# Rows turned into columns by VectorE in blocks of 32, in place of TensorE transposes, in a metaformer layer with routed experts

## The reference, cut to what matters

```python
x = x + conv_attention(layer_norm_over_channels(x))        # 8 images, 64 channels, 256 pixels
t = to_tokens(x)                                           # 2048 tokens of 64 channels
n = layer_norm(t)
probs = softmax(n @ router_w.T)                            # 8 experts
top, idx = top_k(probs, 2); top = top / (top.sum(-1) + 1e-9)
h = silu(n @ w1[e].T) * (n @ w3[e].T)                      # hidden width 682
t = t + sum over the two chosen e of  top * (h @ w2[e].T)
x = from_tokens(t)
```

## Time and profile before

| | us |
|---|---|
| median of 3 runs (lowest, highest) | 174.03 (172.21, 176.63) |
| the profiled execution | 174.15 |
| its span, first to last instruction | 172.4 |
| busy in the span: PE, DVE, ACT, POOL | 146.7, 97.1, 71.4, 86.2 |
| mean granted clock of TensorE, share of full speed | 0.959 |

### The profile page before, as it was taken

One profiled execution on the slowest core, in us unless ns is written; L12 is line 12 of the kernel. 1 busy time (PEld: TensorE's weight loads), 2 busy tenths in 40 slices (PEclk: granted clock), 3 DMA queues, 4 the chain that ended last, 5 costly groups with the idle time before them and its releaser, 6 DMA issues.

```text
span 172.4 us, 4966 instructions
## 1 busy us (share of the span) xinstructions
PE 146.7 (85%) x1725; PEld 119.7 (69%) x1725; DVE 97.1 (56%) x364; ACT 71.4 (41%) x141; POOL 86.2 (50%) x114
## 2 busy tenths in 40 slices
PE   1589889886979899919999999999999999984772
PEld 1356757344446688818898999999999999874262
DVE  1636695884765799828363656455554645433050
ACT  2347666123144352502363636363645454542011
POOL 2695227887777722777262625344443526356000
PEclk9999999998799999985899999999999999999789
DMA  4999200108815955945969795969688930000435
GB/s 135 335 297 302 69 0 19 31 15 268 327 38 99 322 220 201 345 110 162 389 181 378 222 391 148 399 177 364 224 268 319 296 145 30 11 25 19 116 135 122
DMA packets 19894, 33.00 MB, mean 191 GB/s; under 512 B 7692, under 2 KB 13101, under 8 KB 19869
## 3 DMA queue, kind: packets, MB, share of 16 engines
q1 hardware_dynamic: 16732, 29.55, 52.2%
q0 software_dynamic: 2272, 2.35, 4.1%
q10 hardware_dynamic: 864, 0.79, 1.4%
HBM read 25.55 MB, written 7.13 MB: 190 GB/s over the span
## 4 chain that ended last, share of the span: by engine, by line
POOL 35%; issue 32%; PE 11%; DVE 11%; DMA 5%; ACT 3%; POOLq 1%; SPq 0%; DVEq 0%; ACTq 0%
POOL ys L375 21%; POOL xs L366 13%; DMA y_in<-ys 2%; PE psum L1129 2%; DVE hid L833 2%; ACT xn L431 2%; PE psum L934 2%; DVE xrows L638 1%; DMA ys<-y_out,y_row 1%; PE psum L945 1%; PE psum L905 1%; DMA proj<-projections 1%; POOL rstd_t L356 1%; DVE rows L600 1%; PE psum L900 1%
## 5 line engine op out<-in xcount | busy, mean ns | idle before, releaser
L375 POOL DMA_INDIRECT ys<-y_out,y_row x39 | 37.3, 957 | 44.3 <-DVE y_out L845 35.2
L833 DVE TENSOR_TENSOR hid<-psum,act_sb 128x512 f32<-128x512 f32 (+1 forms) x50 | 33.9, 677 | 33.0 <-ACT act_sb L509 32.6
L1056 PE MATMUL psum<-x_cols,weights 64*128 64x128 f32 x390 | 49.6, 279 | 0.4 <-DVE hid L833 0.4
L1058 PE MATMUL psum<-x_cols,weights 64*128 64x128 f32 x390 | 49.7, 279 | 0.0
L1056 PEld LDWEIGHTS psum<-x_cols,weights 64*128 64x128 f32 x390 | 45.5, 187 | 3.9 <-issue 2.6
L1058 PEld LDWEIGHTS psum<-x_cols,weights 64*128 64x128 f32 x390 | 45.6, 187 | 0.0
L366 POOL DMA_INDIRECT xs<-xrows,pos x32 | 32.1, 1003 | 17.5 <-issue 8.7
L509 ACT ACTIVATE act_sb<-psum 128x512 f32<-128x512 f32 (+1 forms) x50 | 29.3, 587 | 25.3 <-PE psum L1056 24.9
L1084 PE MATMUL psum<-hid,weights 128*64 128x128 f32 x468 | 30.6, 287 | 0.0
L1084 PEld LDWEIGHTS psum<-hid,weights 128*64 128x64 f32 x468 | 27.8, 144 | 1.9 <-issue 0.3
L978 PE MATMUL psum<-ones,before 128*128 128x512 bf16 x67 | 18.8, 418 | 3.5 <-issue 3.5
(11 more groups left out here) (147 smaller groups left out, 173.1 us busy)
## 6 DMA issues: line engine op xcount, KB each, us to landing
weights<-experts SPq DMA_DIRECT2D x39, 565.0 KB, 5.5
xs<-zeros SPq DMA_DIRECT2D x4, 1040.0 KB, 11.6
x_in<-xs SPq DMA_DIRECT2D x39, 32.5 KB
ys<-y_out,y_row POOLq DMA_INDIRECT x39
xs<-xrows,pos POOLq DMA_INDIRECT x32, 4.0
y_in<-ys ACTq DMA_DIRECT2D x2, 256.0 KB, 4.6
y_in<-ys SPq DMA_DIRECT2D x2, 256.0 KB, 4.3
x_sb<-x_tok SPq DMA_DIRECT2D x1, 384.0 KB, 3.6
```

The lines of the kernel that those rows point to most:

```text
L375: nc.gpsimd.indirect_dma_start(ys, bass.IndirectOffsetOnAxis(ap=y_row[:, j:j + 1], axis=0), y_out[:, i % RING, h, :], None).then_inc(y_sca ...
L833: nc.vector.tensor_tensor(live(i, hid[:, i % 2, s, :]), live(i, H3_BANK[g % 3]), live(i, act_sb[:, g % 3, :]), ALU.mult).then_inc(hid_done, 1)
L1056: first_ = nc.tensor.matmul(H1_BANK[g % 2][:, src], weights[0:C, slot, P * s:P * (s + 1)], x_cols[0:C, i % 2, src], start=True, stop=True)
L1058: second_ = nc.tensor.matmul(H3_BANK[g % 3][:, src], weights[C:P, slot, P * s:P * (s + 1)], x_cols[C:P, i % 2, src], start=True, stop=True)
```

## The change

Rows are no longer spread over 128 partitions, one row each, but over 32 partitions, four rows each: partition p of a subtile holds rows 4p to 4p + 3, which lie one behind the other in DRAM. `turn_x` is now DVE's: four transposes in 32x32 blocks write the four parts of `x_cols` (two halves of the channels, each twice) straight from `x_in`, and four small copies bring the row numbers of each part to their partitions; in the last phase a predicated copy follows. PE's transposes, ACT's copy, `x_pairs` and `X_BANK` are gone, and with them two filler matmuls. A column of a subtile now stands for another row than before (column 32r + p for row 4p + r), and `occupancy` compares accordingly in four parts.

SP reads four entries of a table with one load, and the order of its DMAs is the same from quad 2 on: table, rows, weights. The turn of quad 2 moves from behind the third product of quad 1 to behind the fifth.

The diff (one line that only drops a bank's name is left out):

```diff
--- before.py
+++ after.py
@@ -54,7 +54,7 @@
 YROWS = PARK + NS * SUB
 WQUADS = 3
 WSLOTS = WQUADS * QUAD
-TURNED_AT = {0: 1, 1: 4}
+FOLD = SUB // 32
 XRING = 4
 RING = 4
 ZW = E * CAP * RW // (QUARTERS * P * 8)
@@ -144,11 +144,11 @@
         jump = sb("jump", [P, E - 1])
         row_at = sb("row_at", [P, NS])
         limit = sb("limit", [P, NS])
-        table = sb("table", [P, 2, NS], I32)
+        table = sb("table", [P, 2, NQ * QUAD], I32)
         keep = sb("keep", [P, NS], I32)
 
-        x_in = sb("x_in", [P, XRING, QUAD, RW])
-        x_pairs = sb("x_pairs", [P, 2, QUAD, 2, C])
+        x_in = sb("x_in", [32, XRING, QUAD, FOLD, RW])
+        ids = sb("ids", [P, NS], I32)
         x_cols = sb("x_cols", [P, 2, QUAD * SUB])
         act_sb = sb("act_sb", [P, 3, BLK])
         hid = sb("hid", [P, 2, STEPS, BLK])
@@ -193,8 +193,8 @@
 
         w_loaded = [sem(f"w_loaded{i}") for i in range(WSLOTS)]
         x_in_loaded = [sem(f"x_in_loaded{i}") for i in range(XRING)]
-        x_paired, y_row_ready, hid_cleared = sem("x_paired"), sem("y_row_ready"), sem("hid_cleared")
-        x_turned, x_cols_ready = sem("x_turned"), sem("x_cols_ready")
+        y_row_ready, hid_cleared = sem("y_row_ready"), sem("hid_cleared")
+        x_cols_ready = sem("x_cols_ready")
         h1_done, h3_done = sem("h1_done"), sem("h3_done")
         silu_done, hid_done, hid_used = sem("silu_done"), sem("hid_done"), sem("hid_used")
         y_copied, y_turned, y_out_ready = sem("y_copied"), sem("y_turned"), sem("y_out_ready")
@@ -278,28 +278,28 @@
                     sp.dma_start(weights[:, slot, :], experts[bass.ds(owners[h], 1)].rearrange("o p c -> p (o c)")
                                  ).then_inc(w_loaded[slot], 16)
 
+            def entries(i, kind, most):
+                quad = table[0:1, kind, QUAD * i:QUAD * i + len(members(i))]
+                return nc.values_load_multi_w_load_instructions(quad, engines=(mybir.EngineType.SP,), min_val=0, max_val=most)[1]
+
             def owners_of(i):
-                return [sp.value_load(table[0:1, 0, QUAD * i + h:QUAD * i + h + 1], min_val=0, max_val=E - 1)
-                        for h in members(i)]
+                return entries(i, 0, E - 1)
 
             def rows_of(i):
-                return [sp.value_load(table[0:1, 1, QUAD * i + h:QUAD * i + h + 1], min_val=0, max_val=E * CAP - SUB)
-                        for h in members(i)]
+                return entries(i, 1, E * CAP - SUB)
 
             def load_rows(i, at):
                 if i >= XRING:
                     sp.wait_ge(y_row_ready, i - XRING + 1)
-                    sp.wait_ge(x_paired, i - XRING + 1)
                 for h in members(i):
-                    sp.dma_start(x_in[:, i % XRING, h, :], xs[bass.ds(at[h], SUB), :]).then_inc(x_in_loaded[i % XRING], 16)
+                    sp.dma_start(x_in[:, i % XRING, h, :, :],
+                                 xs[bass.ds(at[h], SUB), :].rearrange("(p r) c -> p r c", r=FOLD)).then_inc(x_in_loaded[i % XRING], 16)
 
             def landed(p):
                 sp.wait_ge(dispatched[p], 16 * TPP * K_TOP * (KNOWN[p] - (KNOWN[p - 1] if p else 0)))
 
             sp.wait_ge(owners_ready, 1)
-            for h in members(0):
-                owner = sp.value_load(table[0:1, 0, h:h + 1], min_val=0, max_val=E - 1)
-                sp.dma_start(weights[:, h, :], experts[bass.ds(owner, 1)].rearrange("o p c -> p (o c)")).then_inc(w_loaded[h], 16)
+            load_weights(0, owners_of(0))
             sp.wait_ge(table_ready, 1)
             early_rows, second_owners = [rows_of(0), rows_of(1)], owners_of(1)
             landed(0)
@@ -307,18 +307,13 @@
             load_rows(1, early_rows[1])
             load_weights(1, second_owners)
             for p in range(1, PHASES):
-                sp.wait_ge(owners_ready, p + 1)
-                opening = quads_of(p)[0]
-                if opening < WQUADS:
-                    load_weights(opening, owners_of(opening))
                 sp.wait_ge(table_ready, p + 1)
                 for i in quads_of(p):
-                    at = rows_of(i)
-                    if i == opening:
+                    at, owners = rows_of(i), owners_of(i)
+                    if i == quads_of(p)[0]:
                         landed(p)
                     load_rows(i, at)
-                    if i >= WQUADS:
-                        load_weights(i, owners_of(i))
+                    load_weights(i, owners)
 
             all_scattered(sp)
             for q in range(0, QUARTERS, 2):
@@ -399,7 +394,7 @@
             count_up(steps_sub[:], [[SUB, MOST]], SUB, 0)
             for p in range(PHASES):
                 count_up(slot_at[:, OPENED[p]:OPENED[p + 1]], [[SUB, OPENED[p + 1] - OPENED[p]]], 0, 0)
-            count_up(slot_no[:], [[1, 1]], 0, 1)
+            count_up(slot_no[:], [[1, 1]], 0, FOLD)
             count_up(y_row[:], [[SUB, NS]], PARK, 1)
             nc.gpsimd.affine_select(out=upto[:], in_=upto[:], compare_op=ALU.is_ge, fill=0.0, base=0,
                                     pattern=[[1, E], [-1, E]], channel_multiplier=0).then_inc(tables_made, 1)
@@ -494,12 +489,6 @@
                     kq_copy(p + 2)
             nc.scalar.preload_act_table(ACT.Silu)
 
-            def columns(i):
-                act.wait_ge(x_turned, i + 1)
-                if i >= 2:
-                    act.wait_ge(h3_done, STEPS * (i - 1))
-                nc.scalar.copy(live(i, x_cols[:, i % 2, :]), live(i, X_BANK)).then_inc(x_cols_ready, 1)
-
             def silu(g):
                 i, s = divmod(g, STEPS)
                 act.wait_ge(h1_done, g + 1)
@@ -524,14 +513,11 @@
                     ins = nc.scalar.copy(y_cols[0:odd, i % 2, whole:whole + P], Y_BANK[0:odd, whole:whole + P])
                 ins.then_inc(y_copied, 1)
 
-            columns(0)
             for i in range(NQ):
                 if i >= 1:
                     y_copy(i - 1)
                 for s in range(STEPS):
                     silu(STEPS * i + s)
-                    if s == TURNED_AT.get(i, 0) and i + 1 < NQ:
-                        columns(i + 1)
             y_copy(NQ - 1)
             nc.scalar.preload_act_table(ACT.Exp)
             act.wait_ge(shifted, 1)
@@ -727,8 +713,11 @@
                 chain(nc.vector.tensor_reduce(limit[:, own], starts[:, own, :], AX.X, ALU.add))
                 chain(nc.vector.scalar_tensor_tensor(out=limit[:, own], in0=limit[:, own], scalar=left[:, 0:1],
                                                      in1=row_at[:, own], op0=ALU.add, op1=ALU.subtract))
-                nc.vector.tensor_tensor(keep[:, own], limit[:, own], slot_no[:].to_broadcast([P, n]), ALU.is_gt
-                                        ).then_inc(keep_ready, 1)
+                for r in range(FOLD):
+                    part = slice(32 * r, 32 * (r + 1))
+                    nc.vector.scalar_tensor_tensor(out=keep[part, own], in0=limit[part, own], scalar=float(r * (SUB - 1)),
+                                                   in1=slot_no[part, :].to_broadcast([32, n]), op0=ALU.add, op1=ALU.is_gt
+                                                   ).then_inc(keep_ready, 1)
 
             def gate_shifts():
                 dims = [P, TILES, E]
@@ -779,20 +768,26 @@
             x_logits(0)
             scales(3)
 
-            def pair_up(i):
+            def turn_x(i):
                 slot, n = i % XRING, len(members(i))
+                own = slice(QUAD * i, QUAD * i + n)
                 dve.wait_ge(x_in_loaded[slot], landed_in(i))
                 if i >= 2:
-                    dve.wait_ge(x_turned, i - 1)
-                nc.vector.tensor_copy(x_pairs[:, i % 2, 0:n, :, :], x_in[:, slot, 0:n, 0:C].unsqueeze(2)
-                                      .to_broadcast([P, n, 2, C])).then_inc(x_paired, 1)
-                own = slice(QUAD * i, QUAD * i + n)
-                ids = x_in[:, slot, 0:n, ID].bitcast(I32)
-                if own.stop <= OPENED[PHASES - 1]:
-                    nc.vector.tensor_copy(y_row[:, own], ids).then_inc(y_row_ready, 1)
-                else:
-                    dve.wait_ge(keep_ready, 1)
-                    nc.vector.copy_predicated(y_row[:, own], keep[:, own], ids).then_inc(y_row_ready, 1)
+                    dve.wait_ge(h3_done, STEPS * (i - 1))
+                for part in range(4):
+                    c = 32 * (part % 2)
+                    ins = nc.vector.transpose(live(i, x_cols[32 * part:32 * (part + 1), i % 2, :]
+                                                   ).rearrange("p (h r t) -> p h r t", r=FOLD, t=32),
+                                              x_in[:, slot, 0:n, :, c:c + 32])
+                ins.then_inc(x_cols_ready, 1)
+                into = y_row if own.stop <= OPENED[PHASES - 1] else ids
+                for r in range(FOLD):
+                    ins = nc.vector.tensor_copy(into[32 * r:32 * (r + 1), own], x_in[:, slot, 0:n, r, ID].bitcast(I32))
+                if into is ids:
+                    chain(ins)
```

(31 more changed lines are left out.)

## The result

| | median, us | runs | ratio to before, 95% interval |
|---|---|---|---|
| before | 174.56 | 4 (172.21 to 176.63) | |
| after | 178.9 | 4 (177.3 to 178.94) | 1.0282 [1.0225, 1.0339] |

The change makes the kernel 2.8% slower. The median lies in the range that was given (167.5 to 180), but the forecast, 172.8, was a gain, and the result is a loss. The profiled execution took 178.91 us, 176.7 of it span, against 174.15 and 172.4: of the 4.76 us, 4.3 are in the span. In the experiments e2 and e3 the profiled execution was slower than the median (180.19 against 177.51, 180.81 against 179.27), so from those two only instructions, waits and clocks are read.

The account below looks back on a forecast made before the run. The prediction took DVE to bound the first quads and PE the others. A loss of 0.7 to 2.0 us by quad 3, less 2.8 us in the steady quads, gave -1.4 and 172.8 us; range 167.5 to 180.

Parts of the forecast that it names:

- One turn on DVE: Four transposes at 0.60 us and four copies at 0.07 hold DVE 2.70 us, 2.95 from quad 4 on.
- Start of the expert stage: Quad 0: turns 0 and 1 delay the first product by 3.9 us; PE pauses 4 us, then half clock; quad 1 at 71.5.
- The pause of quad 1: DVE's wait for quad 2's rows goes, DVE itself is late next; quad 2 starts at 83.7 against 83.81.
- Quad 2: First product 2.0 us late; 1.3 lost at full clock or 2.6 at half; quad 3 starts 0.7 to 2.0 behind.
- Rival 3: Start of quad 2: its weights, behind table and rows, land last, at worst 2.1 us late: 175 us, chance 0.18.
- The order of the loads: SyncE, quad 2: rows go first, issued 72.0 to 74.0 with no weights ahead, there at 75.4 to 78.7.
- The steady quads: PE drops the 0.49 us turn and DVE's fits its gap: quads 3 to 7 and quad 8 give 2.8 us.
- Sum: Whole kernel: 0.7 to 2.0 lost, less 2.8 gained, is -2.1 to -0.8 us, middle -1.4, so 172.8 us.
- rival 2: DVE transposes slow, 1.14 us each, a turn 4.84: +13.9 us, 188 us; chance 0.12.

Follow-up runs that it names:

- e2: Changed kernel with each copy of row numbers directly behind the transpose that writes the same partitions: 177.51 us, ratio 1.0229.
- e3: Changed kernel with 20 filler matmuls on PE in front of the last rank: 179.27 us, ratio 1.0237.
- e1: Changed kernel with all four transposes of a turn writing partitions 0 to 31, three of them to a spare tile: 178.43 us, ratio 1.0217.
- f4: Changed kernel with 14 filler matmuls on PE before the last step of quad 1's down: 177.35 us, ratio 1.0222.
- f1: Changed kernel with two transposes on DVE, each with its copy behind it, and ScalarE copying the half to the other 64 partitions: 174.52 us, ratio 1.0026.
- g2: f1 with the weights of quad 2 issued ahead of its rows again: 171.55 us, ratio 0.9865.

## Why the prediction was wrong

**The step that failed first is "One turn on DVE", 2.70 us.** It was a sum of durations from start to start, 0.60 and 0.07, that held for instructions which overlap; the eight of a turn don't. Measured: 0.72 for a transpose and 0.18 to 0.22 for a copy in the mean of four, 3.58 to 3.76 in all. The 0.60 itself was right (e1). The forecast said what an error here would cost, but for the transposes alone: 0.1 us on each costs 0.4 in each of the first four turns. By that, 0.12 makes 4 x 4 x 0.12 = 1.9 us, and the copies, which no bound looked at, 4 x 4 x 0.11 = 1.8 more. Against a forecast of -1.4, +3.7 gives +2.3, by the forecast's own sum.

A rule that would have said it was there to read. The Trainium skill, "VectorE: DVE Perf Modes", section "Two Vector instructions with no wait between them", says that an instruction whose output or input starts in another quadrant (32 partitions) than the last one's in the same memory is held, and that "a held instruction starts only when every earlier Vector instruction has finished". The trace agrees: 0.72 held, 0.60 not held. It gives no price; here it is 0.12 us for a transpose and about as much for a copy. Rows of before had even shown it. This is its timeline of DVE, where the two copies into wu_x write from partition 0 and from partition 64:

```profile
10.48 0.23 DVE L769 COPY bias_x<-psum 128x72 f32<-128x72 f32 x1 [1.43 <-PE psum L992]
10.63 0.50 DVE L772 COPY wu_x<-psum 64x80 f32<-64x80 f32 x2
11.16 0.16 DVE L572 SCALAR_TENSOR_TENSOR shift_x<-moments,rstd 128x4 f32<-128x4 f32 x1
```

The copy of 72 columns lets the next start after 0.15; the two of 80 columns hold the engine for 0.53, or 0.27 each. About 0.12 us a hold was to be had from these three lines.

**Start of the expert stage.** Forecast: first product 3.9 late. Measured 5.9 (65.57 against 59.68): two turns at 3.69 and 3.58 instead of 2.70 are the 1.9 between. The pause of PE (4.97, forecast 4) and the half clock in quad 0 came as forecast; up to the first product the clock costs nothing, as e3 shows. Quad 1 at 73.47, forecast 71.5.

**The pause of quad 1.** Its mechanism was right: the rows come in time, the pause goes, DVE itself is late next. Quad 2 started at 86.5, forecast 83.7: three turns' excess, 0.99 + 0.88 + 1.06 = 2.9.

**Quad 2.** Forecast: quad 3 is 0.7 to 2.0 behind. Measured 5.9. Of the 4.5 beyond the middle of that, the four turns make 3.8 (the fourth, 87.99 to 91.58, is 0.89 over), and turn 0 begins 0.24 later. The keep in four parts, which also change quadrants, took 0.79 where 0.18 plus 0.3 was reckoned: 0.3. The half clock came as feared; without it f4's quad gained 0.75. Rival 3 came true in its mechanism: the weights landed last, after a wait of 0.77. It was hidden in great part by late products, and f1 and g2 show what it is worth when they are not late.

**The order of the loads failed too.** The sum of four turns counts each us of a turn as a us of time. The runs bear out about two thirds of that: f1's first four turns are 6.6 us shorter than after's (8.0 against 14.6), and its median is 4.4 us lower, with quad 4's 0.8 back as well. By that the 3.8 us of excess are an estimated 2.5 of the 6.1 us between the forecast and the median. Part of the rest hangs on a term that "The pause of quad 1" put at nothing outside rival 3: what lands behind the rows once they go first. The weights of quad 2 went out at 76.53, 2.5 later than forecast, and the last that PE waited for came at 87.34, where rival 3 had 85.8 at worst; the longest weight transfer took 9.2 us to landing (line 278 by itself), against the 7.4. With the turn short, putting these weights first again gave 1.6% (g2 against f1). How the 6.1 us divide exactly stays open, as no run has a turn of 2.70.

**The steady quads.** Forecast 8.48 each and 2.8 us in all; measured 8.53 to 8.55 and 1.7. That a turn fits into the gap on DVE was nearly wrong: at 3.69 instead of 2.95 (97.45 to 101.14) it lies beyond the gap of 3.1 but inside PE's slack. In quad 4 it doesn't: two operations for the gate shifts stand ahead (105.33 to 105.85), the product comes at 110.14, PE waits for it and the quad takes 9.35; with the shorter turns of e1 and f1 it takes 8.54 and 8.53. That quad lost 0.38 where it was to gain 0.49, which is 0.87 of the 1.1 that are missing.

**Sum.** By the positions in the profile, -1.4, plus 4.5 at quad 3, plus 1.1 in the steady quads is +4.2; the last block's copy is 4.24 late. The other 0.5 of the 4.76 lies outside the span (2.2 us around it, against 1.75). That the time lies in the range is owed to the range's width: neither the forecast nor any rival as priced gives 178.9. The range reached so far because rival 2, the slow turn, had been priced, but as a slow transpose with a chance of 0.12, when what was slow was the succession.

## What to carry to other kernels

Where several instructions of one engine follow each other, price what they hold the engine for in that succession, not one by one: in these runs VectorE's work cut into 32-partition pieces lost about 0.12 us at each change of partitions, and pieces of the same partitions belong next to each other. Moving work from the bound engine to an idle one paid only in the stages where the other was idle: the same edit, kept to the last six quads, where PE was the bound, with each copy behind its transpose and the order of the loads left alone, turned +2.8% into -2.2%. When a wait is shortened and the time stays, look for the next transfer in the same queue before giving up the theory.

## What the runs showed that was not expected

- The cost of a change of partitions applies to an instruction of four elements as much as to one of 512: 0.07 us became 0.18 where each of four copies changes partitions (0.71 for four), and 0.13 in e2, where the copy stays on the partitions of the transpose ahead and only the transpose behind it is held.
- Fillers moved a fall of the clock rather than prevented it: in e3 it was whole where it had been at half, and fell some 8 us later in the same quad, behind a pause of 1.99 us.
- The clock stayed whole in quad 0 of after behind a pause of PE of 1.20 us (68.78) and fell behind one of 1.29 in the kernel before. What tells these apart was not tried.
- ScalarE's copy from 64 partitions to the other 64 took 0.62 us for 512 columns in f1, beside VectorE's work, and so did half the turn for less than the 1.44 us that two transposes take there.
